# The transposed keys are kept in DRAM by groups of four heads, and each store of them becomes four stores

## The reference, cut to what matters

```
state = tanh(p_t + state)                      # 1024 steps, then a gate and a layer norm
q = _rms(heads(wq), qn_w); k = _rms(heads(wk), kn_w); v = heads(wv)
scores = einsum('bhqd,bhkd->bhqk', q, k) * HD ** (-0.5)
scores = where(causal, scores, -inf)
attn = softmax(scores)                         # every query sees all earlier keys of its sequence
x = x + (einsum('bhqk,bhkd->bhqd', attn, v) @ wo.T)   # the first 64 columns set to 0
moe = wts0 * o0 + wts1 * o1 + wts2 * o2 + wts3 * o3   # four networks of the normalized rows
```

## Time and profile before

| | us |
|---|---|
| median of three runs (lowest, highest) | 1571.85 (1570.39, 1574.86) |
| the profiled execution, its own time | 1571.85 |
| its span, from the first to the last instruction | 1569.9 |
| PE busy | 1396.4 (89%) |
| DVE busy | 1096.9 (70%) |
| ACT busy | 882.9 (56%) |
| POOL busy | 311.7 (20%) |

### The profile page before, as it was taken

One profiled execution on the slowest core, in us unless ns is written; L12 is line 12 of the kernel. 1 busy time (PEld: TensorE's weight loads), 2 busy tenths in 40 slices (PEclk: granted clock), 3 DMA queues, 4 the chain that ended last, 5 costly groups with the idle time before them and its releaser, 6 DMA issues.

```text
span 1569.9 us, 33516 instructions
## 1 busy us (share of the span) xinstructions
PE 1396.4 (89%) x12320; PEld 1106.4 (70%) x12320; DVE 1096.9 (70%) x2916; ACT 882.9 (56%) x2042; POOL 311.7 (20%) x1146
## 2 busy tenths in 40 slices
PE   6924789987899799998999999999999999999997
PEld 3413568876788568875878669875788567884797
DVE  6857567655688876668888777778799658783234
ACT  2544546655664685577565772537631686338941
POOL 3333323333233332223323110001000010001000
PEclk9965569998999899998999999999999999999999
DMA  3474555665467557664557647585557566666454
GB/s 107 141 220 149 145 172 154 189 192 157 149 189 211 151 155 218 211 192 129 174 155 205 206 142 202 160 235 181 182 177 229 164 210 205 202 210 200 151 148 131
DMA packets 242738, 278.52 MB, mean 177 GB/s; under 512 B 35600, under 2 KB 166160, under 8 KB 242320
## 3 DMA queue, kind: packets, MB, share of 16 engines
q1 hardware_dynamic: 242576, 276.38, 58.7%
HBM read 234.18 MB, written 43.45 MB: 177 GB/s over the span
## 4 chain that ended last, share of the span: by engine, by line
PE 61%; DVE 14%; ACT 9%; DMA 7%; issue 5%; POOL 2%; SPq 1%; ACTq 0%; DVEq 0%
PE PS L1297 56%; ACT work L1251 4%; PE PS L1300 3%; DMA KT<-ktd 3%; DVE mx L1756 3%; PE PS L1381 2%; POOL AD L1957 2%; DMA WB<-wlo_e_l 1%; ACT PX L1183 1%; DVE st L1574 1%; DVE mxb L1756 1%; POOL work L1964 1%; DMA UU<-in_L_attn_x 1%; DMA WB<-wlo_e_w 1%; ACT L1251 1%
## 5 line engine op out<-in xcount | busy, mean ns | idle before, releaser
L1183 ACT ACTIVATE PX<-AD 128x8 f32<-128x8 f32 x1023 | 219.7, 215 | 253.8 <-POOL AD L1957 252.7
L1957 POOL TENSOR_TENSOR AD<-PX 128x8 f32<-128x8 f32 x1023 | 243.2, 238 | 565.3 <-ACT PX L1183 551.9
L1251 ACT ACTIVATE work<-PS 128x1024 f32<-128x1024 f32 (+1 forms) x312 | 285.9, 959 | 68.2 <-PE PS L1297 67.0
L1756 DVE TENSOR_REDUCE mx<-PS 128x2 f32<-128x1024 f32 (+3 forms) x256 | 256.2, 1019 | 58.4 <-PE PS L1297 57.8
L1297 PE MATMUL PS<-work,vlx 128*32 128x256 f32 (+2 forms) x2816 | 241.6, 384 | 19.3 <-POOL work L1964 6.2
L1297 PE MATMUL PS<-EP,u_e_l 128*128 128x256 f32 x1024 | 195.8, 285 | 7.2 <-DMA WB<-wlo_e_l 3.6
L1276 ACT ACTIVATE work<-PS 128x512 f32<-128x512 f32 x176 | 102.4, 593 | 173.9 <-PE PS L1297 173.4
L1297 PE MATMUL PS<-WB,work 128*128 128x192 f32 x1024 | 184.7, 335 | 5.1 <-ACT work L1276 2.0
L1964 POOL TENSOR_SCALAR_AFFINE_SELECT work<-work 128x512 f32<-128x512 f32 x96 | 63.8, 676 | 619.5 <-ACT work L1251 619.4
L1297 PE MATMUL PS<-EP,WB 128*128 128x256 f32 x640 | 180.1, 281 | 0.0
L1297 PEld LDWEIGHTS PS<-WB,work 128*128 128x128 f32 x1024 | 168.9, 193 | 10.3 <-issue 4.6
(11 more groups left out here) (170 smaller groups left out, 2243.4 us busy)
## 6 DMA issues: line engine op xcount, KB each, us to landing
KT<-ktd SPq DMA_DIRECT2D x112, 512.0 KB, 4.3
WB<-wlo_e_l SPq DMA_DIRECT2D x160, 256.0 KB, 4.0
ktd<-KTs SPq DMA_DIRECT2D x32, 512.0 KB, 4.3
WB<-wlo_e_up SPq DMA_DIRECT2D x64, 256.0 KB, 3.6
WB<-wlo_e_w SPq DMA_DIRECT2D x64, 256.0 KB, 3.2
WB<-wdn_e_down SPq DMA_DIRECT2D x64, 192.0 KB, 3.2
KT<-ktd SPq DMA_DIRECT2D x48, 256.0 KB, 3.4
KT<-ktd SPq DMA_DIRECT2D x32, 384.0 KB, 3.9
```

What stands on the lines that cost most here:

```text
L1183: eng.activation(cur, AD[n % 2], ACT.Tanh).then_inc(of(*key), 1)
L1251: eng.activation(pt[:, :, :, q0:L], two("sc", *a).rearrange("p a (l q) -> p a l q", l=2)[:, :, :, q0:L], ACT.Exp).then_inc(of(*key), 1)
L1756: eng.tensor_reduce(o, two("mxm", *a)[:, :, 0:w], AX, ALU.max, negate=True).then_inc(of(*key), 1)
L1957: eng.tensor_tensor(AD[n % 2], PX[c % 2][:, :, :, t], PX[(n - 1) // L % 2][:, :, :, (n - 1) % L], ALU.add).then_inc(of(*key), 1)
```

## The change

Three things are changed together. The tensor ktd gets a dimension of four groups ahead of the partitions, so that the two planes of a group lie in 1 MB of their own, with 8 KB from one partition to the next in place of 32 KB. Each `kst` becomes four DMAs of 128 KB, one for each group, which all count on the semaphore of the kst, by 64 in all. And the loads take their group from the new place; their sizes, runs and buffers stay as they were.

```
-        return {"vst": 64, "mtd": 32}.get(key[0], 16)
+        return {"vst": 64, "kst": 64, "mtd": 32}.get(key[0], 16)
...
-        ktd = dram("ktd", (B, 128, 8, T))
+        ktd = dram("ktd", (B, 4, 128, 2, T))
...
                     sp.wait_ge(*done("kc", *a))
-                    eng.dma_start(ktd[b, :, :, 128 * t:128 * t + 128], plain(KTs)).then_inc(of(*key), 16)
+                    for g in range(4):
+                        eng.dma_start(ktd[b, g, :, :, 128 * t:128 * t + 128],
+                                      plain(KTs[:, 2 * g:2 * g + 2, :])).then_inc(of(*key), 16)
...
-                            eng.dma_start(plain(keys_of(kt[:, 512 * i:], 2, n)), ktd[b, :, 2 * g:2 * g + 2, 0:n]).then_inc(of(*key), 16)
+                            eng.dma_start(plain(keys_of(kt[:, 512 * i:], 2, n)), ktd[b, g, :, :, 0:n]).then_inc(of(*key), 16)
...
-                                      ktd[u % B, :, 2 * g + planes[0]:2 * g + planes[-1] + 1, 0:n]).then_inc(of(*key), 16)
+                                      ktd[u % B, g, :, planes[0]:planes[-1] + 1, 0:n]).then_inc(of(*key), 16)
...
-                                      ktd[u % B, :, 2 * g:2 * g + 2, 512 * h:512 * h + n]).then_inc(of(*key), 16)
+                                      ktd[u % B, g, :, :, 512 * h:512 * h + n]).then_inc(of(*key), 16)
```

## The result

The changed kernel takes 1583.9 us in the median of six runs (1580.8 to 1590.1), the kernel before 1573.5 us in six runs beside it (1570.4 to 1579.6). The ratio is 1.0072 with a 95% interval of 1.0041 to 1.0101: slower by 0.7%, some 10 to 11 us. The forecast was 1573.9, its range ended at 1582, and "slower by over 0.3%" had a chance of 0.26. The forecast was wrong.

The account below looks back on a forecast made before the run. PE's row of work was taken as the bound; 1.0 (179 us) + 0.3 (532 us) + 0.5 (small things) + 0.2 (landing) = 2.0 us on 1571.85 gave 1573.9 us, own range 1570 to 1577, 8-in-10 range 1568 to 1582.

Parts of the forecast that it names:

- What bounds the kernel: PE's row of work sets the end; SP or DMA changes count only where PE runs into them.
- More issuing on SP: Four stores take SP 2.04 us, not 0.56; what stands behind a store comes 0.7 to 1.48 us later, taken as 0.9.
- The landing of the store: Four stores land 0.5 us later, lengthening SP's 7 waits before loads of keys; costed at 0.2 us, 3.5 without cover.
- The two places where SP meets PE: Behind the stores at 179.01 and 531.96 us PE waits longer: 1.0 us and 0.3 us.
- The layout for the loads: Loads of keys at 8 KB pitch in place of 32 KB: cost 0, bounds +0 and -8 us.
- B: Rival: SP's delay behind the 19 stores that waited for ScalarE reaches PE; 1578.3 to 1587.2 us, chance 0.26.
- A: Rival: the 32 KB pitch was slow, so each load of keys lands sooner, -7.7 us; 1566.2 us, chance 0.08.

Follow-up runs that it names:

- e1: Kernel before with its layout kept (32768 B pitch), only each store split into four of 128 KB: 1571.16 us, ratio 1.0004.
- e2: Changed kernel with 256 B of padding behind a partition's two planes (8448 B pitch, no merging): 1573.65 us, ratio 1.0001.
- e5: Changed kernel with a group's two planes in different megabytes, 8192 B pitch kept, no merging: 1582.63 us, ratio 1.0067.
- e6: Changed kernel with 128 B behind each plane, so rows still merge but at 8448 B pitch: 1577.07 us, ratio 1.0030.
- e8: Kernel before with six long-satisfied semaphore waits on SP behind each two-plane load of keys: 1571.43 us, ratio 1.0005.
- e11: Kernel before with ten long-satisfied semaphore waits on SP behind each two-plane load of keys: 1572.42 us, ratio 0.9994.
- e10: Changed kernel with planes outside the partitions: 4096 B pitch, a group's planes 512 KB apart, no merging: 1580.73 us, ratio 1.0040.
- e3: Changed kernel's merging layout, but two unmerged stores per tile, one per plane, in place of four: 1580.75 us, ratio 1.0071.
- e9: Changed kernel with two groups to a row: 16384 B pitch, no merging, four stores: 1574.44 us, ratio 1.0013.
- e4: Kernel before with 256 B of padding per partition, so its one store no longer merges into 1024 rows: 1570.81 us, ratio 0.9991.

## Why the prediction was wrong, point by point

**What bounds the kernel**: right. PE's row of work sets the end; the loss is PE at rest for DMAs.

**More issuing on SP**: the forecast of 2.04 us for four stores held where they are not merged (1.96 in e1), and fell short in the kernel itself (2.55), since I took vd<-Vs as the nearest row and did not see that the new stores would be merged. The stall behind the large store went (1.79 to 1.09 us), as said. "I take 0.9" for the delay of what stands behind a store was about right: in e1 the loads behind the store at 179 us start 1.2 us later than before, counted from the store (3.67 against 2.47 us), and the three DMAs behind the one at 532 us are done 0.6 us later (4.00 against 3.44). The 2.0 us of the whole sum can't be told from nothing in e1 (1.0004, up to 1.0022).

**The landing of the store**: I had added 0.5 us to each of SP's waits for it. They became shorter instead, 17.5 us in all in the earlier trace rows and now 8.4. This alone does not say that the stores land sooner: SP spends some 2 us more on the issuing of each and comes to the wait that much later.

```profile
SPq L1120 <- DMA ktd<-KTs: 6.4, 7, 1.9
...
SPq L1118 <- DMA ktd<-KTs: 2.0, 2, 1.6
```

The formula that the prediction takes from the Trainium skill for the landing is given there for DMAs issued by GpSimd; these are SP's, and what counts for them are the measured 3.5 and 2.5 us.

**The two places where SP meets PE.** At 183 us I forecast 3.5 us of idle time in place of 2.52, and got it in e1 (3.52). The kernel after shows this, 0.8 us more, of which the merged stores make 0.6 (2.55 against 1.96):

```profile
185.28 1.12 PE L1299 MATMUL PS<-QT,KT 64*128 64x128 f32 x8 [4.33 <-issue]
```

At 532 us the store, the load and the product that waits are these in the kernel after (SP, then PE), to be set against the earlier trace rows:

```profile
537.18 2.54 SPq L1107 DMA_DIRECT2D ktd<-KTs  x4
539.76 0.62 SPq L1120 DMA_DIRECT2D KT<-ktd  x1
```

```profile
545.09 0.69 PE L1299 MATMUL PS<-KT,QT 64*128 64x384 f32 x2 [3.45 <-DMA KT<-ktd]
```

From the start of the store to the product:

| | store to issue of load | load to product | sum | PE idle for it |
|---|---|---|---|---|
| before | 0.61 | 5.22 | 5.83 | none |
| e1 (four stores) | 2.02 | 4.48 | 6.50 | 0.75 |
| e2 (layout, padded) | 2.03 | 4.19 | 6.22 | 0.46 |
| e5 (8192 B) | 2.01 | 5.04 | 7.05 | 1.30 |
| e6 (merged) | 2.59 | 4.88 | 7.47 | 3.00 |
| after | 2.58 | 5.33 | 7.91 | 3.45 |

The forecast was +0.3 us here. The split alone gives +0.7, since half of SP's delay comes back: issued 1.4 us later the load needs 0.7 us less to the product, as the forecast had it, with most of the store's bytes gone. The layout triples it to +2.1. This is one place; it shows how each part arrives at PE, not how often.

**The layout for the loads: this is the step that failed.** "I see no price of the pitch, and cost the layout at 0. Bounds: +0, and -0.7 us for each of the 11 waits, -8." The size was wrong, and so was the bound, which allowed only a gain. Two mistakes are in it. First, I compared stores (ktd<-KTs and gd<-work) to learn what loads would do. Stores showed no price of the pitch and still show none (e5's of 128 KB land in 2.2 us, e1's in 2.4). The trace of before had loads with the new layout's steps: G<-gd, whose partitions are 8 KB apart and twice its plane step. Its row on SP's timeline of before, with the loads of keys of the same shape ahead of it:

```profile
155.71 2.93 SPq L1116 DMA_DIRECT2D KT<-ktd  x6
158.69 0.47 SPq L1094 DMA_DIRECT2D x1d<-XR  x1
159.19 1.26 SPq L1082 DMA_DIRECT2D G<-gd  x2
```

That is 0.6 us for each of two against 0.49 for each of six, and it would have given the merging its price. Second, I took "their number, bytes, runs and buffers are the same" for "the loads are the same". By the medians the 112 loads of 512 KB became 0.7 us slower each and the 112 smaller ones 0.3, together 112 us of later landing; load by load between the two traces it is 80 us. Of that 19 us came through to the end in this execution, and 10 to 11 us in the usual one, one part in four to eight. Even the mirror image of my own bound, +8 on the 2 of the rest, would have reached no further than 1581.9 (1571.85 + 2 + 8), within the 1582 of the range, since it counted only the 11 waits that were there; the kernel after has 17.

**The rivals.** B forecast the right side and nearly the right time (1578 to 1587) for the wrong reason: SP's delay behind the stores, which e1 shows to cost nothing, as e8 and e11 do for a delay between the loads. A named the right mechanism, a pitch that slows the transfers, with the wrong sign: it took 32768 B for the bad pitch, and of those tried 8192 B is the one that is shown to cost time. The Trainium skill ("DMA: Bandwidth & Descriptors", latency and other measured facts) has copies slow down at large powers of two between rows; its figures begin at 512 KiB. The runs show a loss at 8192 B, gone with 256 B of padding, and none at 32768 B; within this kernel the measurement decides.

**What stays open**: why 8192 B between 128 partitions slows loads and 32768 B does not; what part of e5's loss is its planes' distance of exactly 1 MB, which no run tries without the pitch, and so whether the two effects really fail to add up (0.67% and 0.30%, together 0.72%); why 16384 B slows the one-plane loads nearly as much as 8192 B does, and not those of two planes; and what part of e10 is its 4096 B. None of the versions is faster than the kernel before beyond its interval; the changed layout is free with padding (e2) and gains nothing.

## What to carry to other kernels

A new layout of a DRAM buffer is a change to every DMA that reads it, even where bytes, runs and count are the same: ask for its pitch from partition to partition and whether two of its dimensions now merge, and look in the trace for a transfer in the same direction that already has these steps. If none is there, bound the term on both sides, and by the number of loads that could become waits, not by those that wait today. A few hundred bytes of padding per partition are a cheap second version to time beside the plain one. A delay on an issuing queue that mostly waits for other engines may cost nothing at all, even where one place shows it in full.

## What the runs showed of the hardware that was not expected

- A load of 384 KB into 128 partitions, one run of 3 KB for each, with 8192 B from run to run landed in 4.1 us, with 32768 B in 3.2 and with 8448 B in 3.0 (the same load in e5, before and e2); 16384 B gave 3.9. Over all 64 loads of one run of 3 or 4 KB the median loss at 8192 and at 16384 B was 0.4 to 0.5 us (e5, e3, after; e9).
- A two-plane load whose memory side merges into 256 rows: issued in 0.56 to 0.61 us and not 0.37 to 0.47, and landed 0.4 us later (4.1 against 3.7) at the same bytes; its first packet moved 1.3 us behind the issue and not 1.0. A store that merges into 1024 rows is issued in 0.57 us, unmerged in 0.37 (e4).
- Ten waits that had long been satisfied, behind each load, widened the distance of loads on SP from 0.49 to 0.65 us (2.93 to 3.92 us for six), and the kernel's time did not move.
